# Moving the dense query product and splitting off the output gate in a two-pass attention kernel

## The reference

```
q1 = (x @ Wq) * scale ; k1 = x @ Wk ; v = x @ Wv
q2 = (x @ Wqa @ Wqb) * scale ; k2 = softmax((x @ Wka @ Wkb) per head)
gk1, gk2 = log_sigmoid(x @ Wg?a @ Wg?b + bg?) / 16
e = softmax(x @ We) ; mask = one_hot(top 1) ; rw = e * mask
o = gla(q1, k1, v, gk1) + sum over experts gla(q2 rw, k2 rw, v, gk2 mask)
g = x @ Wga @ Wgb
o = rmsnorm(o) * norm_w * (g * sigmoid(g)) ; out = o @ Wo
```

## Time and profile before

| | us |
|---|---|
| median of 3 timed runs | 2491.58 (2491.54 to 2492.33) |
| the profiled execution | 2488.14 |
| its span, first to last instruction | 2486.3 |
| TensorE busy (share of the span) | 2398.0 (96%) |
| VectorE busy | 1849.6 (74%) |
| ScalarE busy | 1553.4 (62%) |
| GpSimd busy | 1137.7 (46%) |

### The profile page before, as it was taken

How to read it: one execution, slowest core, us unless ns; L and a number is a source line. 1 busy time by engine, 2 the same in 40 slices (tenths; PEclk the granted TensorE clock), 3 DMA queues, 4 the chain that set the end, 5 groups by cost and what they waited for, 6 DMA issues and landing times. The chain is left out here.

```text
span 2486.3 us, 56360 instructions
## 1 busy us (share of the span) xinstructions
PE 2398.0 (96%) x20208; PEld 1423.2 (57%) x20208; DVE 1849.6 (74%) x3484; ACT 1553.4 (62%) x3281; POOL 1137.7 (46%) x929
## 2 busy tenths in 40 slices
PE   5999999998999999999999999999999999999997
PEld 2444444454666666666666666666666666666654
DVE  5444444426888888888888888888888888888885
ACT  3222322236777777777777777777777777777773
POOL 2587533314444444444444444444444444444444
PEclk9999999998999999999999999999999999999999
DMA  5634434311111111111111111111111111111111
GB/s 140 200 103 121 103 101 102 83 52 39 48 46 45 44 42 42 42 42 42 48 45 51 42 47 43 42 42 42 42 46 46 51 42 46 42 42 42 42 26 35
DMA packets 250704, 145.65 MB, mean 59 GB/s; under 512 B 208096, under 2 KB 208096, under 8 KB 250144
## 3 DMA queue, kind: packets, MB, share of 16 engines
q1 hardware_dynamic: 240048, 119.32, 19.3%
q10 hardware_dynamic: 9504, 17.31, 1.9%
q0 software_dynamic: 1104, 8.40, 0.9%
HBM read 61.09 MB, written 33.55 MB: 38 GB/s over the span
## 5 line engine op out<-in xcount | busy, mean ns | idle before, releaser
L319 PE MATMUL psum<-wb,region 128*128 128x512 f16 x768 | 293.1, 382 | 0.0
L320 PE MATMUL psum<-wb,region 128*128 128x512 f16 x768 | 292.3, 381 | 0.0
L321 PE MATMUL psum<-wb,region 128*128 128x512 f16 x768 | 292.2, 380 | 0.0
L1058 POOL TENSOR_TENSOR region<-region,kfac 128x512 f32<-128x512 f32 x64 | 66.7, 1042 | 455.4 <-DVE kfac L1313 455.4
L1041 POOL TENSOR_TENSOR region<-region 128x1024 f32<-128x1024 f32 x64 | 147.8, 2309 | 260.0 <-DVE region L1419 231.5
L1419 DVE SCALAR_TENSOR_TENSOR region<-psum,region 128x512 f16<-128x512 f32 x64 | 44.3, 692 | 223.6 <-ACT region L868 223.6
L1046 POOL TENSOR_TENSOR region<-region 128x1024 f32<-128x1024 f32 x64 | 150.6, 2353 | 92.2 <-DVE region L1190 92.2
L1053 POOL TENSOR_SCALAR region<-region,m 128x512 f32<-128x512 f32 x256 | 172.3, 692 | 25.6 <-DVE hm L1261 25.6
L586 PE MATMUL psum<-region 128*128 128x512 f16 x768 | 176.2, 379 | 2.1 <-DVE region L1419 2.1
L1069 POOL TENSOR_TENSOR region<-region,decay 128x512 f32<-128x512 f32 x64 | 67.2, 1049 | 201.9 <-DVE decay L1330 201.9
L1224 DVE SCALAR_TENSOR_TENSOR region<-psum,m,region 128x512 f32<-128x512 f32 x192 | 144.2, 751 | 6.8
(11 more groups left out here) (232 smaller groups left out, 7327.4 us busy)
## 6 DMA issues: line engine op xcount, KB each, us to landing
region<-x_in SPq DMA_DIRECT2D x128, 256.0 KB, 2.6
q_cols<-region ACTq DMA_DIRECT2D x64, 256.0 KB, 2.5
region<-q_cols SPq DMA_DIRECT2D x64, 256.0 KB, 2.8
out_rows<-region SPq DMA_DIRECT2D x62, 256.0 KB, 2.0
region<-wb_in POOLq DMA_DIRECT2D x1, 3072.0 KB, 13.8
region<-wqkv_in SPq DMA_DIRECT2D x4, 512.0 KB, 6.1
region<-region SPq DMA_TRANSPOSE x128, 3.0
region<-ws_in POOLq DMA_DIRECT2D x1, 1280.0 KB, 6.7
```

Of the source, the lines that this page charges most:

```text
L319: mm(out, lhs(0), rhs(0), start=start, stop=False)
L320: mm(out, lhs(0), rhs(1), start=False, stop=False)
L321: return mm(out, lhs(1), rhs(0), start=False, stop=stop)
```

## The change

On TensorE the dense query product `project_q1` moves from behind `cumulate` to directly in front of `project_k2`, and from bank 5 to bank 6. The output gate's second stage leaves `gates` and becomes `out_gate`, behind `project_k2`, in bank 1. The dense cumulated gates go to bank 5 instead of bank 1. `out_mm` of tile n - 2 comes behind `cumulate` and no longer before it. On ScalarE and VectorE the log gates are worked on over 1024 columns, and the output gate apart over 512: three more instructions on ScalarE (`front_out_gate`, behind `front_sig_high`) and one more on VectorE (`front_out_logsig`, behind `front_lslow`). `front_ke` moves behind them, `front_logsig` in front of `front_kmax`, `front_ksum` behind `front_out_logsig`. Three semaphores are new (`og_pe`, `kw_pe`, `ls3_ok`, and `og_log_ok`, which counts three steps a tile). The diff, without the two lists of semaphore names:

```
...
@@ -233,7 +233,7 @@
                              q_p[bass.ds(j, 1), p, :, :].rearrange("a p c -> (a p) c")).then_inc(S(f"qb{p}_in"), 16)
 
             def turn_xn(n):
-                wait_alone(sp, S("q1_pe"), prev(n))
+                wait_alone(sp, S("kw_pe"), prev(n))
                 wait_alone(sp, S("xn_ok"), cur(n))
                 sp.dma_start_transpose(xnT.rearrange("p x a b -> p (x a) b"), xn.rearrange("p x c -> p (x c)")).then_inc(S("xnT_in"), 16)
 
@@ -371,9 +371,13 @@
                 pe.wait_ge(S("low_ok"), cur(n))
                 pe.wait_ge(S("am1_ok"), prev(n))
                 pe.wait_ge(S("am2_ok"), prev(n))
-                for k, which in ((0, 1), (1, 1), (2, 0)):
-                    last = second(bank[4 + k], which, k)
+                for k in range(2):
+                    last = second(bank[4 + k], 1, k)
                 last.then_inc(S("g_pe"), 1)
+
+            def out_gate(n):
+                pe.wait_ge(S("v_ok"), cur(n))
+                second(bank[1], 0, 2).then_inc(S("og_pe"), 1)
 
             def wide(n, where, w0, done):
                 for g in range(KT):
@@ -401,15 +405,15 @@
                 if back:
                     pe.wait_ge(S("sel_ok"), (n - 1) * 4 + 4)
                 for g in range(KT):
-                    mm3(bank[2], lambda x: xnT[:, x, g, :], lambda x: wb[:, x, g, C:2 * C], g == 0, g == KT - 1)
+                    last = mm3(bank[2], lambda x: xnT[:, x, g, :], lambda x: wb[:, x, g, C:2 * C], g == 0, g == KT - 1)
+                last.then_inc(S("kw_pe"), 1)
 
             def project_q2(n):
                 pe.wait_ge(S("ls_ok"), cur(n))
                 second(bank[4], 2, 3).then_inc(S("q2_pe"), 1)
 
             def project_q1(n):
-                pe.wait_ge(S("ls_ok"), cur(n))
-                wide(n, 5, 0, "q1_pe")
+                wide(n, 6, 0, "q1_pe")
 
             def cumulate(n, back):
                 pe.wait_ge(S("v_ok"), cur(n))
@@ -421,11 +425,11 @@
                 pe.wait_ge(S("kd_ok"), cur(n))
                 pe.wait_ge(S("carry_ok"), prev(n))
                 for gate, weights, done in ((0, centred16[:, :], "cum1_pe"), (1, same_d[:, :], "cum_pe")):
-                    mm(bank[1 + 2 * gate], weights, ls16[:, 0, gate, :], start=True, stop=False)
-                    mm(bank[1 + 2 * gate], weights, ls16[:, 1, gate, :], start=False, stop=True).then_inc(S(done), 1)
+                    mm(bank[5 - 2 * gate], weights, ls16[:, 0, gate, :], start=True, stop=False)
+                    mm(bank[5 - 2 * gate], weights, ls16[:, 1, gate, :], start=False, stop=True).then_inc(S(done), 1)
 
             def half_sums(n):
-                pe.wait_ge(S("e1_ok"), cur(n))
+                pe.wait_ge(S("sil_ok"), cur(n))
                 for pr in range(PAIRS):
                     f = slice(pr * P, (pr + 1) * P)
                     for x in range(2):
@@ -533,17 +537,19 @@
                     inter_dense(m, front)
                     intra(m, mp)
                 if front:
+                    project_q1(n)
                     project_k2(n, back)
+                    out_gate(n)
                     project_k(n, back)
                 if first:
                     pe.wait_ge(S("same_ok"), cur(n))
                 if ahead:
                     den(n + 2, p, b, back=back)
+                if front:
+                    cumulate(n, back)
                 if tail:
                     out_mm(t, back)
                 if front:
-                    cumulate(n, back)
-                    project_q1(n)
                     project_q2(n)
                     half_sums(n)
                 if ahead:
@@ -740,15 +746,26 @@
                 ac(lexp[:, :], ldiff[:, :], ACT.Exp, scale=1.0 / W_SCALE, accum_out=lsum[:, :]).then_inc(S("lexp_ok"), 1)
 
             def front_gates(n, part):
+                logs = gch[:, 0:2 * C]
                 if part == 1:
                     act.wait_ge(S("abs_ok"), cur(n))
-                    ac(gch, gch, ACT.Exp, scale=-1.0).then_inc(S("ex_ok"), 1)
+                    ac(logs, logs, ACT.Exp, scale=-1.0).then_inc(S("ex_ok"), 1)
                     act.wait_ge(S("ex_ok"), cur(n))
-                    ac(gch, gch, ACT.Ln, bias=1.0).then_inc(S("ln_ok"), 1)
+                    ac(logs, logs, ACT.Ln, bias=1.0).then_inc(S("ln_ok"), 1)
                     return
                 act.wait_ge(S("g_pe"), cur(n))
                 act.wait_ge(S("ls_ok"), prev(n))
-                ac(gch, psum[:, 4:7, :].rearrange("p a b -> p (a b)"), ACT.Abs).then_inc(S("abs_ok"), 1)
+                ac(logs, psum[:, 4:6, :].rearrange("p a b -> p (a b)"), ACT.Abs).then_inc(S("abs_ok"), 1)
+
+            def front_out_gate(n):
+                gate = gch[:, 2 * C:]
+                act.wait_ge(S("og_pe"), cur(n))
+                act.wait_ge(S("ls3_ok"), prev(n))
+                ac(gate, bank[1], ACT.Abs).then_inc(S("og_log_ok"), 1)
+                act.wait_ge(S("og_log_ok"), n * 3 + 1)
+                ac(gate, gate, ACT.Exp, scale=-1.0).then_inc(S("og_log_ok"), 1)
+                act.wait_ge(S("og_log_ok"), n * 3 + 2)
+                ac(gate, gate, ACT.Ln, bias=1.0).then_inc(S("og_log_ok"), 1)
 
             def front_sig_high(n):
                 act.wait_ge(S("ls_ok"), cur(n))
@@ -756,6 +773,7 @@
                    scale=LS_SCALE).then_inc(S("lsh_ok"), 1)
 
             def front_sig(n):
+                act.wait_ge(S("ls3_ok"), cur(n))
                 ac(logsig[:, 2, :], logsig[:, 2, :], ACT.Exp).then_inc(S("sig_ok"), 1)
 
             def front_v(n, p):
@@ -770,8 +788,8 @@
                 act.wait_ge(S("cum1_pe"), cur(n))
                 act.wait_ge(S("tr_pe"), n * 4 + 1)
                 act.wait_ge(S("u_pe"), prev(n))
-                ac(ep1, bank[1], ACT.Exp, scale=1.0 / LS_SCALE)
-                ac(em1, bank[1], ACT.Exp, scale=-1.0 / LS_SCALE).then_inc(S("e1_ok"), 1)
+                ac(ep1, bank[5], ACT.Exp, scale=1.0 / LS_SCALE)
+                ac(em1, bank[5], ACT.Exp, scale=-1.0 / LS_SCALE).then_inc(S("e1_ok"), 1)
                 act.wait_ge(S("cum_pe"), cur(n))
                 ac(ep2, bank[3], ACT.Exp, scale=1.0 / LS_SCALE)
                 ac(em2, bank[3], ACT.Exp, scale=-1.0 / LS_SCALE).then_inc(S("e2_ok"), 1)
@@ -825,11 +843,12 @@
                     front_gates(n, 0)
                     front_router(n)
                     front_gates(n, 1)
-                    front_ke(n)
                 if back:
                     back_square(m)
                 if front:
                     front_sig_high(n)
+                    front_out_gate(n)
+                    front_ke(n)
                     front_sig(n)
                 if ahead:
                     ahead_z(n + 2)
@@ -1106,8 +1125,7 @@
 
             for b in range(BATCH):
                 last = nc.gpsimd.memset(kacc[b], 0.0)
-            last.then_inc(S("kacc_zero"), 1)
-            pool.wait_ge(S("kacc_zero"), 1)
+            then_step(last)
             for t in range(ALL):
                 add_keys(t, t // TILES)
                 if t in (3, 5):
@@ -1277,15 +1295,19 @@
             def front_logsig(n):
                 dve.wait_ge(S("ln_ok"), cur(n))
                 dve.wait_ge(S("sum_pe"), prev(n))
+                ve.scalar_tensor_tensor(flat(logsig[:, 0:2, :]), psum[:, 4:6, :].rearrange("p a b -> p (a b)"), 0.0, gch[:, 0:2 * C],
+                                        ALU.min, ALU.subtract).then_inc(S("ls_ok"), 1)
+
+            def front_out_logsig(n):
+                dve.wait_ge(S("og_log_ok"), n * 3 + 3)
                 dve.wait_ge(S("sil_ok"), prev(n))
-                ve.scalar_tensor_tensor(flat(logsig), psum[:, 4:7, :].rearrange("p a b -> p (a b)"), 0.0, gch,
-                                        ALU.min, ALU.subtract).then_inc(S("ls_ok"), 1)
+                ve.scalar_tensor_tensor(logsig[:, 2, :], bank[1], 0.0, gch[:, 2 * C:], ALU.min, ALU.subtract).then_inc(S("ls3_ok"), 1)
 
             def front_sil(n, p, again):
                 dve.wait_ge(S("sig_ok"), cur(n))
                 if again:
                     dve.wait_ge(S("ogf_ok"), n)
-                ve.tensor_tensor(sil[:, p, :], bank[6], logsig[:, 2, :], ALU.mult).then_inc(S("sil_ok"), 1)
+                ve.tensor_tensor(sil[:, p, :], bank[1], logsig[:, 2, :], ALU.mult).then_inc(S("sil_ok"), 1)
 
             def front_lslow(n):
                 dve.wait_ge(S("lsh_ok"), n + 1)
@@ -1315,7 +1337,8 @@
             def front_gated_1(n):
                 dve.wait_ge(S("e1_ok"), cur(n))
                 dve.wait_ge(S("q1_pe"), cur(n))
-                ve.scalar_tensor_tensor(q1g, bank[5], D2 ** -0.5 / W_SCALE, ep1, ALU.mult, ALU.mult).then_inc(S("q1g_ok"), 1)
+                dve.wait_ge(S("kw_pe"), cur(n))
+                ve.scalar_tensor_tensor(q1g, bank[6], D2 ** -0.5 / W_SCALE, ep1, ALU.mult, ALU.mult).then_inc(S("q1g_ok"), 1)
                 ve.scalar_tensor_tensor(k1g, bank[2], 1.0 / W_SCALE, em1, ALU.mult, ALU.mult).then_inc(S("k1g_ok"), 1)
 
             def front_gated_q2(n):
```

(5 more changed lines are left out.)

41 lines of the change are left out of this document (24 added, 17 removed).

## The result

The changed kernel takes 2513.38 us (median of 4 runs, 2511.36 to 2513.92), the kernel before 2491.56 (4 runs): the ratio is 1.0087, with a 95% interval of 1.0075 to 1.0100. It is 21.8 us slower. The forecast had the sign and its range holds the time, but the likeliest value, 2497.0, is 16 us short.

What follows compares the result with a forecast made beforehand. A closed loop through VectorE and ScalarE was taken to bound the kernel. Steady tiles 59 x 0.19 = +11.2 us, first and last tiles -5.8: +5.4 on the median 2491.58 gives 2497.0, range 2478 to 2515.

Steps and rivals of the forecast that it cites:

- rival B: Waits pile up on VectorE: 0.45 us a tile, 26.6 - 5.8 = +20.8 us, 2512; chance 0.14.
- B's two delays: Key maximum waits 0.15 to 0.2 us for the product behind the dense query, and output-gate logs are late as well.
- The hole in TensorE is slack of the loop, not its cause: TensorE's 0.60 us hole at the low-rank key is slack; VectorE and ScalarE close the 29.65 us loop.
- rival A: TensorE is the bound: a tile would take its stream of 29.05 us, 41.2 us saved with the ends, 2450; chance 0.14.
- The loop grows by 0.19 us: ScalarE's exponentials start at 1354.12 instead of 1353.93, behind subtraction, sigmoid and normaliser: 59 x 0.19 = +11.2 us.
- The collision stays: VectorE's L1176 still loses to GpSimd's L1062, ending 1.81 us after GpSimd's start; 0.48 us of lateness swallowed except for 0.19.
- B's first delay: VectorE's key maximum waits 0.15 to 0.2 us for the product behind the dense query.
- its second, late gate logs: ScalarE's output-gate logs, expected with 0.01 us to spare, reach VectorE late.
- First and last tiles: Shorter waits in the first two tiles (3.4 us) and the last two (2.4 us), together -5.8 us.
- the three chances: Chances of the measured time: slower than 2496.6, 0.48; within 5.0 us of no change, 0.34; faster than 2486.6, the remainder.
- C: Little moves: the loop grows by 0.10 us or less and the ends give 6, 2491 to 2492; chance 0.12.
- only count if the exponentials can use it: Low part of the gates done 1.1 us earlier, so TensorE's cumulating product is not late; ScalarE's exponentials cannot use this.

Runs made afterwards that it cites:

- experiment 1: Kernel before with two more TensorE products (0.43 us) per tile behind the half sums, at the head of y_mm: 2516.96 us, ratio 1.0101.
- experiment 6: Changed kernel with TensorE's order as before, so only the output gate is split off: 2510.97 us, ratio 1.0079.
- experiment 7: Kernel before with two more TensorE products (0.43 us) per tile directly ahead of the state's dense products: 2490.61 us, ratio 0.9996.
- experiment 3: Kernel before with VectorE's low half of the normed rows issued behind its gated products: 2490.69 us, ratio 0.9998.
- freeing the port: Changed kernel with VectorE's low half of the normed rows issued behind its three gated products, no longer before them: 2455.79 us, ratio 0.9858.
- experiment 8: Changed kernel with VectorE's sum of squares put in front of the key maximum: 2494.44 us, ratio 1.0010.
- experiment 4: Changed kernel with the out product back ahead of the cumulated gates on TensorE: 2477.11 us, ratio 0.9944.
- experiment 10: Changed kernel with the out product back ahead of the cumulated gates and VectorE's low half of the normed rows behind the gated products: 2487.27 us, ratio 0.9989.
- experiment 5: Changed kernel with ScalarE's Ln and Exp of the normaliser put before the sigmoid's Exp: 2559.18 us, ratio 1.0270.

## Why the prediction was half right

The range held the time, but not for the reasons given: it was stretched to the price of rival B, 2512, and that price came within 2 us of the time while only one of B's two delays happened. So much is luck.

*"The hole in TensorE is slack of the loop, not its cause": wrong.* The kernel before has two loops of nearly the same length. The first goes low-rank key, TensorE until the low-rank products of the next tile, ScalarE's copies of them, VectorE from the router to the selection, low-rank key. Experiments 1, 6 and 7 show its extent, 3 and 6 that it holds the tile when VectorE loses nothing to a collision. I saw no idle note on VectorE and ScalarE from one end to the other and took that for proof that they alone close the loop. The sign that I passed over is in ScalarE's rows. Before, the first low-rank copy (L729) starts 1.04 us after the start of the two copies ahead of it; after the change, where TensorE is early, 0.95. In the kernel before it waited 0.09 us for TensorE, too little for a note; in experiments 1 and 3 the same wait is long enough to be listed.
```profile
1365.26 1.06 ACT L686 ACTIVATE region<-psum 128x512 f32<-128x512 f32 x2
1366.30 0.38 ACT L729 ACTIVATE region<-psum 64x256 f16<-64x256 f32 x1
```
```profile
1375.33 1.06 ACT L692 ACTIVATE region<-psum 128x512 f32<-128x512 f32 x2
1376.28 0.37 ACT L735 ACTIVATE region<-psum 64x256 f16<-64x256 f32 x1
```
So the second loop was 29.55 us, the first 29.64. The change did remove the first (12 products were put ahead of the key, 2 behind it), which is why freeing the port pays only there. The argument against rival A used the missing idle notes, and the rule of the Trainium skill that I set aside with it (Perfetto Trace Analysis, Identifying Performance Opportunities: close the gaps of the most-contended engine) names the right place: with both loops cut, TensorE's stream sets the time, 2455.8 where A gave 2450 (the stream is 29.17 us, not the 29.05 that I worked out). The gap alone was not enough.

*"The loop grows by 0.19 us": right mechanism, term too small.* On a clock that starts with VectorE's first instruction of the tile the exponentials started at 16.27 before, I had them at 16.46, and they started at 16.61. The chain is the one described: subtraction, sigmoid, normaliser, exponentials. The 0.15 are the wait at the key maximum, which I bounded and then took at nothing; experiment 8 shows that it counts. It cost 0.25, and 0.11 of that was made up ahead of it: the join (L1247) started 9.13 into the tile, where L1229 of before had started at 9.24. Why the join came earlier the runs do not show.

*"The collision stays": right, and again too small.* I counted the lost time as GpSimd's start and 1.81 us. L1194 ended 2.07 us after it, because GpSimd's product itself took 0.25 longer: it began while L1183, also with two SBUF inputs, was running (until 1366.28), and ended 1.13 us after that; alone it takes 1.27. No run takes L1183 away alone, but the tiles of this kernel vary it: in every second one L1183 starts 0.10 earlier, GpSimd's product starts at the same place, and it ends 0.10 earlier. The next tile, with VectorE's first instruction at 1377.29:
```profile
1395.64 0.69 DVE L1183 TENSOR_TENSOR region<-region 128x512 f16<-128x512 f32 x1
```
```profile
1396.04 1.42 POOL L1081 TENSOR_TENSOR region<-region 128x512 f32<-128x512 f32 x1 [1.65 <-ACT region L795]
```
In experiments 4 and 10, where L1183 is long over, it takes 1.27 to 1.28; in experiment 5 the order is turned round and L1183 is the one that takes 0.95 longer. Together L1194 ends 0.58 us later in the tile shown than before, and 0.49 in every second tile, instead of 0.19. Of that 0.09 come back at the low-rank copies, and the average tile is 0.45 longer, the value of rival B. B's first delay came true (0.17); its second, late gate logs, did not; the 0.25 on the port stood in its place.

*The rule on the port* (the Trainium skill, SBUF — State Buffer, Who interferes with whom) held wherever the stamps of the two were 0.05 us or more apart: experiments 4, 5, 6 and 10 agree. Nearer than that GpSimd also won with the later stamp.

*First and last tiles:* 3.6 us came back where I had 5.8.

*Small slips:* the three chances do not add up as written: with 0.26 of the forecast, nearly all of C's 0.12 and a little of A, "within" is nearer 0.38 and "faster" nearer 0.14. And the low-rank key is two products (L367, L368), so four low-rank products stand ahead of the key projection and not three; the second stage of the gates has four in all, in three lines. No term of the sum hangs on this.

*The cumulated gates "only count if the exponentials can use it":* right. In experiment 4 they come 2.6 us later and the kernel is faster.

## What to carry to other kernels

An engine whose rows show no idle note can still be held, by waits too short for a note. Whether a wait is slack or cause is found out by adding work on either side of it: here 0.43 us a tile cost 26.6 us on one side and nothing on the other. When two loops are nearly equal, removing one pays only with the other, so a change that measures worse can be the needed half of a good one: this one needed a single call moved on another engine. And where two engines share a port, the place of an instruction on it is right only for one timing; moved 1.6 us, the cure became the collision.

## What the runs showed that I had not expected

- Later exponentials made the kernel faster: 1.6 us later in the tile, 36 us less in all (experiment 4).
- The collision also works the other way within one chain: a VectorE product of 0.69 us lengthened GpSimd's 1.27 to 1.52, which then lengthened the next VectorE one from 0.75 to 1.76.
- Near a tie the stamps decide at a sharp edge. In the kernel before VectorE's low half was at most 0.03 us ahead of GpSimd's product in 59 tiles and lost 58 of them; 0.04 ahead it won 21 of 25 (experiments 1 and 7), and from 0.05 ahead on it won every time (experiments 4 and 6).
